# Batch norm and GELU per output block beside the matmuls, and a first expert search with two score buffers and indices in two halves

## The chip, the cores and the metric

The kernel runs on one NeuronCore of a Trainium2 chip. The metric is the device time of one execution in microseconds (us). TensorE (PE) does matmuls and transposes, VectorE (DVE) element work, maxima and index searches, ScalarE (ACT) activations and copies out of PSUM, GpSimd (POOL) issues the row gathers, and SyncE (SP) the plain transfers.

## The reference, cut to what matters

A graph of 1250 nodes with 512 features goes through four steps, each added to its input. The first two are where the change lies:

```python
# x: (1250, 512)
# 1: graph convolution, batch norm over the nodes, exact GELU
h = segment_sum(norm * (layernorm(x) @ W.T)[row], col) + b
h = (h - mean(h, 0)) * rsqrt(var(h, 0) + eps) * gamma + beta
x = x + gelu(h) + layernorm(x)
# 2: product-key experts, 8 heads, 256 + 256 keys, top 8
q1, q2 = halves of (layernorm(x) @ Wq + bq) per head
s1t, i1 = top_k(q1 @ keys1.T, 8);  s2t, i2 = top_k(q2 @ keys2.T, 8)
scores, best = top_k(all 64 sums of s1t and s2t, 8)
indices = i1 * 256 + i2 at best                 # 64 per node
vals = relu(x . w_down[indices]) * softmax(scores)
x = x + sum(vals * w_up[indices])
# 3: another graph convolution, 4: one of 8 matrices per node
```

## The kernel before, in words

The nodes are ten tiles of 128 rows (the last has 98). The engines run five hand-written programs, each in its own fixed order, which wait for each other through counting semaphores.

The graph convolution keeps its result transposed: `outT` has four blocks of 128 features (`o` = 0 to 3), each 1250 nodes wide. PE first makes four scaled sums `aggT` (four passes over the adjacency counts `AT`, L1312), then multiplies them by the weights, block by block, into one of two accumulators `acc` (L1357). ACT moves a whole block from PSUM to `outT` and adds the bias (L631); DVE takes the batch statistics (L931, L933). When all four blocks have them, the scale and the bias of the batch norm are worked out for the four at once (L934 to L944).

Between the sums and the blocks there is side work: DVE takes the self loops out of the ten tiles of `AT` (L925), ACT turns them into 16-bit copies `few` (L625, L627). On ACT this stands ahead of the first block's L631.

GELU runs by node tile: ACT computes four 128x128 pieces (L642) into `gt` or `diag`, PE flips them into a bank `TK` (L1367), DVE adds the bank to `x` (L950). Tile 0 goes first. Then comes the first search, with nothing between: the layer norm of tile 0 (`y`, L958 to L661), its flip, queries (`Q`, L1385), scores (`S`, L1396), copies of the scores to SBUF by ACT (L682), the eight largest and their places on DVE (L1003, L1008), and for all eight heads together the 64 sums, their best eight, and the 64 row numbers `idx` (L1017 to L1056), then the softmax. There is one score buffer `S` in PSUM for all heads, and two copies in SBUF (`sca`, `pick`). GELU of tiles 1 to 9 follows, after the search on all of ACT, PE and DVE.

The gathers are POOL's: for each tile 32 groups of two, each gather 128 rows of 4 KB out of `in_wdu` (L511). The ring has room for 11 groups; a slot is free again when PE has used it. POOL waits for the tile's `idx` before the first group. For each group DVE multiplies the rows with `y` (L1116), ACT makes a diagonal matrix of the result (L736), PE sums up (L1433). The search of tile 1 is laid over the groups of tile 0 by the table `FIRST`: its statistics, layer norm and queries begin after all ten tiles have their GELU, and its indices come in front of DVE's group 25. Those of the later tiles are laid over earlier groups of the tiles before, two ahead.

Of the kernel before, what the change touches and what calls it, by code (L numbers as in the profile page):

```python
# [111 lines left out]
def lay_out(nc, ctx, k):  # L112
    def sb(name, cols, dt=F32, rows=P):
        return ctx.enter_context(nc.sbuf_tensor(name, [rows, cols], dt))
# [155 lines left out]
    k.few0 = k.wide[:, 0:NPAD // 2].bitcast(I16)  # L270
    k.Y = [banks[2], banks[5]]
    k.O = [k.tr[0][:, :], k.tr[1][:, :]]

def program(nc, x_d, src_d, dst_d, w0t_d, par_d, wq_d, keys_d, wdu_d, w1_d, b1_d, we_d, out_d):
    k = Net()
    with ExitStack() as ctx:
# [3 lines left out]
        def sem(name):  # L283
            return ctx.enter_context(nc.semaphore(name))
# [185 lines left out]
def pool_program(pool, k):  # L470
# [90 lines left out]
def act_program(act, k):  # L561
# [72 lines left out]
    act.activation(k.bsd[:, :], k.bmv[:, FT:2 * FT], ACT.Sqrt, bias=k.eps[:, :]).then_inc(k.bnsd_ready, 1)  # L634
    act.wait_ge(k.bn_ready, 1)


    def gelu(i, par):
        if i > 1:
            act.wait_ge(k.tk_ready, i - 1)  # L640
        for o in range(FT):
            ins = act.activation(k.gtt[par][:, o * P:(o + 1) * P], k.outT[:, o * NPAD + i * P:o * NPAD + (i + 1) * P],  # L642
                                 ACT.Gelu, bias=k.bsc[:, FT + o:FT + o + 1], scale=k.bsc[:, o:o + 1])
        ins.then_inc(k.gelu_done, 1)

# [58 lines left out]
    def search_step(i, at, g):  # L704
        if g == at.y_root:
            y_root(i)
        if g == at.y_norm:
            y_norm(i)
        if g == at.y_copy:
            copy_yT(i)  # L710
        if g == at.y_keep:
            keep_y(i)
        if g in at.q_copy:
            copy_q(i, at.q_copy.index(g))
        if g in at.s_copy:
            copy_scores(i, at.s_copy.index(g))
        if g == at.exps:
            exps(i)
# [18 lines left out]
                                     scale=k.inner[:, j:j + 1])  # L737
            ins.then_inc(k.diag_ready, 1)

    gelu(0, 0)  # L740
    for g in range(FIRST.y_root, FIRST.exps + 1):
        search_step(0, FIRST, g)
    for i in range(1, NT):
        gelu(i, i % 2)
    for g in range(FIRST.y_root, 0):
        search_step(1, FIRST, g)
    for i in range(NT):
# [27 lines left out]
def dve_program(dve, k):  # L775
# [142 lines left out]
    for f in range(FT):  # L918
# [4 lines left out]
    for t in range(NT):  # L923
        loops = k.AT[:, t * NPAD + t * P:t * NPAD + (t + 1) * P]
        dve.tensor_tensor(loops, loops, k.ident[:, :], ALU.subtract).then_inc(k.unlooped, 1)  # L925
    dve.memset(k.outT[:, :].rearrange("p (o c) -> p o c", c=NPAD)[:, :, N:NPAD], 0.0)
    bmv = k.bmv[:, :].rearrange("p (c o) -> p o c", c=2)
    for o in range(FT):
        dve.wait_ge(k.outT_done, o + 1)
        for c, (c0, n) in enumerate(CHUNKS):  # L930
            dve.bn_stats(k.bst[:, (o * 3 + c) * 6:(o * 3 + c + 1) * 6], k.outT[:, o * NPAD + c0:o * NPAD + c0 + n])  # L931
        dve.drain()
        dve.bn_aggr(bmv[:, o, :], k.bst[:, o * 18:(o + 1) * 18])  # L933
    dve.drain().then_inc(k.bnvar_ready, 1)  # L934
    dve.wait_ge(k.bnsd_ready, 1)
    dve.reciprocal(k.bsd[:, :], k.bsd[:, :])
    dve.wait_ge(k.par_in, 16)
    dve.drain()
    dve.tensor_tensor(k.bsc[:, 0:FT], k.bsd[:, :], k.par[:, FT:2 * FT], ALU.mult)
    dve.drain()  # L940
    dve.tensor_tensor(k.bsc[:, FT:2 * FT], k.bsc[:, 0:FT], k.bmv[:, 0:FT], ALU.mult)
    dve.drain()
    dve.tensor_tensor(k.bsc[:, FT:2 * FT], k.par[:, 2 * FT:3 * FT], k.bsc[:, FT:2 * FT], ALU.subtract)
    dve.drain().then_inc(k.bn_ready, 1)  # L944


    def add_gelu(i, par):
        dve.wait_ge(k.tk_ready, i + 1)
        tile = k.x[:, i * D:(i + 1) * D]
        dve.tensor_tensor(tile, tile, k.TK[par], ALU.add).then_inc(k.x1_done, 1)  # L950

    add_gelu(0, 0)
    dve.memset(k.tmv[:, :], 1.0)
    dve.drain()

# [114 lines left out]
    def search_step(i, at, g):  # L1070
        if g == at.y_stats:
            y_stats(i)
        if g == at.y_inv:
            y_inv(i)
        if g in at.maxes:
            maxes(i, at.maxes.index(g))
        if g in at.finds:
            finds(i, at.finds.index(g))
        if g == at.sums:
            sums()  # L1080
        if g == at.best:
            best()
        if g == at.place:
            place()
        if g == at.codes:
            codes()
        if g == at.match:
            match()
        if g == at.rows:
            rows()  # L1090
        if g == at.index:
            index(i)
        if g == at.softmax:
            softmax(i)
# [24 lines left out]
                    accum_out=k.inner[:, j:j + 1])  # L1119
            ins.then_inc(k.inner_ready, 1)  # L1120

    for g in range(FIRST.y_stats, FIRST.softmax + 1):
        search_step(0, FIRST, g)
    for i in range(1, NT):
        add_gelu(i, i % 2)
# [125 lines left out]
def pe_program(pe, k):  # L1251
# [88 lines left out]
    for f in range(1, FT):  # L1340
        if f >= 2:
            pe.wait_ge(k.aggT_done, f - 1)
        for t in range(NT):
            for c0, n in CHUNKS:
                ins = piece(f, f % 2, t, c0, n)
        ins.then_inc(k.agg_ready, 1)

    pe.wait_ge(k.w_in, 16)
    for o in range(FT):
        pe.wait_ge(k.aggT_done, FT - 1 if o == 0 else FT)  # L1350
        if o >= 2:
            pe.wait_ge(k.outT_done, o - 1)
# [6 lines left out]
        ins.then_inc(k.out_ready, 1)  # L1359


    def flip_gelu(i, par):
        pe.wait_ge(k.gelu_done, i + 1)
        if i > 1:
            pe.wait_ge(k.x1_done, i - 1)
        for o in range(FT):
            ins = pe.transpose(k.TK[par][:, o * P:(o + 1) * P], k.gtt[par][:, o * P:(o + 1) * P], ident)  # L1367
        ins.then_inc(k.tk_ready, 1)

    flip_gelu(0, 0)  # L1370
# [69 lines left out]
    for g in range(FIRST.y_flip, FIRST.scores[-1] + 1):  # L1440
        search_step(0, FIRST, g)
    for i in range(1, NT):
        flip_gelu(i, i % 2)
# [93 lines left out]
```

## Time and profile before

| | |
|---|---|
| median of three runs | 1358.37 us (1356.52 to 1358.50) |
| the profiled execution | 1359.03 us, span 1357.2 us |
| PE busy | 1161.3 us, 86% of the span |
| DVE busy | 943.7 us, 70% |
| ACT busy | 520.7 us, 38% |
| POOL busy | 654.3 us, 48% |
| mean granted clock of PE | 0.966 of full |

A row of a timeline gives the start, the busy time, the engine, the line of the program, what is written and read, and in brackets the idle time ahead of it with what ended it. Matmuls in 32 bit show as two records each, and the busy time of a merged row reaches from its first start to its last end.

### The profile page before, as it was taken

How to read it: one execution, taken by the hardware profiler on the slowest of the kernel's cores; microseconds unless marked ns; L12 is line 12 of the kernel's file. 1: busy time of each engine (PE TensorE's matmuls, PEld its weight loads, DVE VectorE, ACT ScalarE, POOL GpSimd, SP SyncE). 2: the span in 40 equal slices, each digit the busy share in tenths (PEclk: the TensorE clock that was granted, in tenths of full speed). 3: DMA queues.
4: the chain of work that ended last, by engine and by line, in shares of the span. 5: the costliest groups of instructions: out<-in, count | busy, mean ns of one | idle time of the engine just before them, and what ended most of it. 6: DMA issues, size and time to landing. Idle time of an engine off the chain costs nothing.

```text
span 1357.2 us, 16428 instructions
## 1 busy us (share of the span) xinstructions
PE 1161.3 (86%) x3844; PEld 566.4 (42%) x3845; DVE 943.7 (70%) x2771; ACT 520.7 (38%) x1280; POOL 654.3 (48%) x706
## 2 busy tenths in 40 slices
PE   0788889996499999899898999989999799889098
PEld 0444445554254444444444444444444233334043
DVE  4777785022669997887978879788797866665211
ACT  1677730053644544344344444434443333320010
POOL 2000000000376677777777776777767777530212
PEclk9999999997599999999999999999999999999599
DMA  8400000000399999999999999999999999943443
GB/s 344 171 1 0 1 1 0 0 0 0 125 410 409 370 409 409 410 408 409 409 408 410 409 409 409 409 409 409 409 409 401 410 409 409 406 159 144 181 149 117
DMA packets 105765, 378.76 MB, mean 279 GB/s; under 512 B 11824, under 2 KB 11826, under 8 KB 104536
## 3 DMA queue, kind: packets, MB, share of 16 engines
q0 software_dynamic: 94720, 343.40, 63.7%
q1 hardware_dynamic: 10968, 34.48, 6.9%
q8 instruction: 30, 0.49, 0.1%
q14 instruction: 47, 0.39, 0.1%
HBM read 359.53 MB, written 19.41 MB: 279 GB/s over the span
## 4 chain that ended last, share of the span: by engine, by line
PE 44%; DVE 15%; DMA 13%; POOL 11%; issue 8%; ACT 5%; DVEq 4%; ACTq 0%; POOLq 0%; SPq 0%
PE tr L1433 17%; DMA AT<-in_wdu,idx 7%; POOL big L511 6%; PE acc L1312 6%; DMA big<-in_wdu,idx 4%; PE acc L1292 4%; POOL AT L511 4%; PE acc L1410 4%; PE acc L1385 3%; DVE big L1116 3%; PE tr L1484 3%; PE tr L1460 3%; DVE outT L846 2%; PE acc L1396 2%; DVE AT L1116 2%
## 5 line engine op out<-in xcount | busy, mean ns | idle before, releaser
L511 POOL DMA_INDIRECT big<-in_wdu,idx x466 | 439.8, 944 | 500.5 <-DVE idx L1056 348.8
L1433 PE MATMUL tr<-big,diag 128*128 128x512 f32 x932 | 434.1, 602 | 34.1 <-ACT diag L736 33.7
L736 ACT ACTIVATE diag<-ident,inner 128x128 f32<-128x128 f32 x640 | 221.6, 393 | 472.0 <-DVE inner L1116 470.6
L1116 DVE CUSTOM_DVE_ANT_0 big<-big,acc,prob 128x512 f32<-128x512 f32 x466 | 327.6, 742 | 79.7 <-DMA big<-in_wdu,idx 78.4
L1433 PEld LDWEIGHTS tr<-big,diag 128*128 128x128 f32 x932 | 168.5, 190 | 258.1 <-issue 166.9
L511 POOL DMA_INDIRECT AT<-in_wdu,idx x174 | 168.7, 970 | 61.6 <-issue 48.7
L1433 PE MATMUL tr<-AT,diag 128*128 128x512 f32 x348 | 163.3, 602 | 8.9 <-ACT diag L736 8.8
L1292 PE MATMUL acc<-outT,diag 128*128 x612 | 120.4, 347 | 40.3 <-DVE outT L846 18.7
L1116 DVE CUSTOM_DVE_ANT_0 AT<-AT,acc,prob 128x512 f32<-128x512 f32 x174 | 122.4, 742 | 33.5 <-DMA AT<-in_wdu,idx 33.1
L846 DVE TENSOR_SCALAR outT<-big 128x1280 f16 x204 | 98.0, 548 | 34.8 <-PE acc L1292 30.0
L1433 PEld LDWEIGHTS tr<-AT,diag 128*128 128x128 f32 x348 | 62.7, 190 | 90.5 <-issue 62.2
L1292 PEld LDWEIGHTS acc<-outT,diag 128*128 x612 | 59.2, 97 | 98.3 <-issue 74.0
L1385 PEld LDWEIGHTS acc<-yT,qk 128*128 128x128 f32 x640 | 81.6, 202 | 19.7 <-issue 17.5
L1385 PE MATMUL acc<-yT,qk 128*128 128x128 f32 x640 | 84.4, 288 | 2.4 <-ACT yT L657 1.4
L1312 PE MATMUL acc<-AT,big 128*128 128x512 f32 (+1 forms) x240 | 84.6, 513 | 0.0
L580 ACT ACTIVATE gt<-big 128x128 f16 x204 | 64.7, 387 | 19.4 <-PE acc L1292 13.6
L1410 PE MATMUL acc<-wide,h1bc 128*128 128x512 f32 (+1 forms) x144 | 61.3, 521 | 4.3 <-issue 4.2
L1396 PE MATMUL acc<-qk,qT 64*128 64x256 f32 x320 | 57.9, 439 | 4.5 <-ACT sca L682 2.3
L1312 PEld LDWEIGHTS acc<-AT,big 128*128 128x128 f32 x240 | 45.4, 190 | 37.9 <-issue 37.3
L1116 DVE DVE_READ_ACCUMULATOR2_ANT inner<- 128x1 f32 x640 | 52.7, 82 | 0.0
L1235 DVE TENSOR_SCALAR pick<-x 128x1 int32<-128x1 f32 x14 | 2.2, 154 | 72.7 <-PE tr L1484 72.7
L1410 PE MATMUL acc<-wide,gt 128*128 128x512 f32 (+1 forms) x96 | 43.2, 544 | 9.4 <-issue 4.9
(234 smaller groups left out, 1056.5 us busy)
## 6 DMA issues: line engine op xcount, KB each, us to landing
sorted_rows<-big SPq DMA_DIRECT2D x8, 1280.0 KB, 17.4
big<-in_we SPq DMA_DIRECT2D x8, 1024.0 KB, 15.1
big<-in_wdu,idx POOLq DMA_INDIRECT x466, 10.6
x<-sorted_rows SPq DMA_DIRECT2D x14, 512.5 KB, 3.4
AT<-in_wdu,idx POOLq DMA_INDIRECT x174, 10.8
x<-in_x SPq DMA_DIRECT2D x1, 2304.0 KB
qk<-in_wq SPq DMA_DIRECT2D x1, 2048.0 KB, 19.8
big<-in_w0t SPq DMA_DIRECT2D x1, 1024.0 KB, 27.5
```

The lines of the kernel that those rows point to most:

```text
L511: pool.indirect_dma_start(out=k.slot[r * GS + s], out_offset=None, in_=k.wdu_d, in_offset=bass.IndirectOffsetOnAxis(ap=k.idx[i % 2][:, j:j ...
L580: act.activation(k.far[:, bass.ds(half + b * P, P)], k.iota[:, NPAD + t * P:NPAD + (t + 1) * P], ACT.Abs, bias=k.neg[:, bass.ds(q * BPS + ...
L736: ins = act.activation(k.diag[:, c * P:(c + 1) * P], k.ident[:, :], ACT.Relu, scale=k.inner[:, j:j + 1])
L846: dve.tensor_scalar(k.ohs[:, bass.ds(half + c * NPAD, NPAD)], k.iota[:, t * P:t * P + NPAD], k.key[:, bass.ds(q * BPS + c, 1)], None, ALU. ...
L1116: ins = dve.tensor_tensor_reduce(out=row, in0=row, in1=k.Y[i % 2], scale=k.prob[:, (i % 2) * HK + j:(i % 2) * HK + j + 1], scalar=0.0, op0 ...
L1292: ins = pe.matmul(acc[:, c0:c0 + n], k.ohb[:, bass.ds(quarter + b * P, P)], k.ohs[:, bass.ds(half + b * NPAD + c0, n)], start=begin and b ...
L1312: return pe.matmul(k.acc[s][:, c0:c0 + n], k.h0[:, t * D + f * P:t * D + (f + 1) * P], k.AT[:, t * NPAD + c0:t * NPAD + c0 + n], start=(t ...
L1385: ins = pe.matmul(k.Q[:, (h % 4) * P:(h % 4 + 1) * P], k.wq[:, f * H * P + h * P:f * H * P + (h + 1) * P], k.yT[:, f * P:(f + 1) * P], sta ...
L1396: ins = pe.matmul(k.S[:, c, 0:NK], k.qT[half, (h % 4) * P:(h % 4 + 1) * P], k.keys[half, h * NK:(h + 1) * NK], start=True, stop=True)
L1410: ins = pe.matmul(k.G[n % 2 if n >= TWO_BANKS else 0][:, 0:cols], k.h1[j % 3][:, f * P:(f + 1) * P], k.wide[:, at:at + cols], start=(j == ...
L1433: ins = pe.matmul(k.O[i % 2], k.diag[:, c:c + P], row, start=(g == 0 and s == 0), stop=(g == NG - 1 and s == GS - 1))
L1460: ins = pe.matmul(k.tr[t % 2][:, :], k.agg1[:, f * NPAD + t * P:f * NPAD + (t + 1) * P], k.w1[f], start=(f == 0), stop=(f == FT - 1))
```

## The change

It does six things.

1. The self loops are taken out of tile t as soon as PE's last pass over `AT` is through with that tile (semaphore `at_free`), not after all passes.
2. ACT moves each block out of PSUM in three chunks (512, 512 and 226 nodes), each released by its own matmuls; DVE takes the statistics of each as it comes.
3. Scale and bias of the batch norm are worked out for each block by itself, and GELU is applied to the whole block in place, 1280 wide. For the last block, GELU is cut into tile 0, tiles 1 to 3 and tiles 4 to 9.
4. PE flips blocks 0 to 2 of tiles 0 to 3 into four banks (`early`) before the last block is finished, and the last block after it. Tiles 4 to 9 are flipped after the first search, with no GELU left to do there.
5. In the first search, even heads use `S` and the copy by ACT, odd heads the new `S1` (two other banks), which DVE reads from PSUM directly. Queries and scores alternate, two heads at a time.
6. The indices of the first search come in two halves (`first_half`): heads 0 to 3 before DVE begins with heads 4 to 7. POOL starts its first 16 groups on the first half. The softmax input moves behind the second half.

```diff
     for i in range(NT):
-        pool.wait_ge(k.idx_ready, i + 1)
         for g in range(NG):
+            if g == 0:
+                pool.wait_ge(k.idx_ready, i + 2 if i else 1)
+            if i == 0 and g == NG // 2:
+                pool.wait_ge(k.idx_ready, 2)
...
-    for o in range(FT):
-        act.wait_ge(k.out_ready, o + 1)
-        act.activation(k.outT[:, o * NPAD:o * NPAD + N], k.acc[o % 2][:, 0:N], ACT.Identity,
-                       bias=k.par[:, o:o + 1]).then_inc(k.outT_done, 1)
-    act.wait_ge(k.bnvar_ready, 1)
+    def out_row(o):
+        for c, (c0, n) in enumerate(CHUNKS):
+            act.wait_ge(k.out_ready, 3 * o + c + 1)
+            act.activation(k.outT[:, o * NPAD + c0:o * NPAD + c0 + n], k.acc[o % 2][:, c0:c0 + n], ACT.Identity,
+                           bias=k.par[:, o:o + 1]).then_inc(k.outT_done, 1)
+        act.wait_ge(k.bnvar_ready, o + 1)
+        act.activation(k.bsd[:, o:o + 1], k.bmv[:, FT + o:FT + o + 1], ACT.Sqrt,
+                       bias=k.eps[:, :]).then_inc(k.bnsd_ready, 1)
+        act.wait_ge(k.bn_ready, o + 1)
+
+    def gelu(o, i0, i1):
+        piece = k.outT[:, o * NPAD + i0 * P:o * NPAD + i1 * P]
+        act.activation(piece, piece, ACT.Gelu, bias=k.bsc[:, FT + o:FT + o + 1],
+                       scale=k.bsc[:, o:o + 1]).then_inc(k.gelu_done, 1)
+
+    for o in range(FT - 1):
+        out_row(o)
+        gelu(o, 0, NT)
+    out_row(FT - 1)
+    gelu(FT - 1, 0, 1)
+    gelu(FT - 1, 1, 4)
+    gelu(FT - 1, 4, NT)
...
+    def unloop(t):
+        if t < NT - 1:
+            dve.wait_ge(k.at_free, t + 1)
...
+    y_stats(0)
+    y_inv(0)
+    for i in range(1, 4):
+        add_gelu(i)
+    first_pair(0)
+    first_pair(2)
+    first_half(0)
+    first_pair(4)
+    first_pair(6)
+    first_half(1)
...
+    softmax(0)
+    for i in range(4, NT):
+        add_gelu(i)
...
+    def first_scores(h):
+        pe.wait_ge(k.qT_done, h + 1)
+        if h == 1:
+            pe.wait_ge(k.x1_done, 4)
+        elif h % 2:
+            pe.wait_ge(k.topk_done, h - 1)
+        elif h:
+            pe.wait_ge(k.sc_ready, h // 2)
...
+    for c in range(4):
+        queries(0, c)
+        first_scores(2 * c)
+        first_scores(2 * c + 1)
+    pe.wait_ge(k.gelu_done, FT + 2)
+    for i in range(4, NT):
+        pe.wait_ge(k.x1_done, max(i - 1, 4))
+        flip_gelu(i, k.TK[i % 2], range(FT)).then_inc(k.tk_ready, 1)
     pe.wait_ge(k.x1_done, NT)
```

ACT at the last block, before (L631 is the move out of PSUM, L634 the root, L642 GELU, L649 the root of tile 0's layer norm):

```order
L631 ACTIVATE outT<-acc,par 128x1250 x4
L634 ACTIVATE bsd<-bmv,eps 128x4
L642 ACT_TABLE_LOAD
L642 ACTIVATE gt<-outT,bsc 128x128 x4
L649 ACT_TABLE_LOAD
```

ACT at the same place of the changed program (L638, L641, L647 and L660 answer to them):

```order
L638 ACTIVATE outT<-acc,par 128x512 x2
L638 ACTIVATE outT<-acc,par 128x226
L641 ACT_TABLE_LOAD
L641 ACTIVATE bsd<-bmv,eps 128x1
L647 ACT_TABLE_LOAD
L647 ACTIVATE outT<-outT,bsc 128x128
L647 ACTIVATE outT<-outT,bsc 128x384
L647 ACTIVATE outT<-outT,bsc 128x768
L660 ACT_TABLE_LOAD
```

GELU and its table loads moved ahead into the blocks; the nine tiles' GELU that stood behind the first search is gone there. Both the root and GELU now need a table load in each of the last three blocks.

DVE in the first search, before: the tail of the last head (L1003, L1008), the index work for eight heads (L1017 to L1056), and the nine additions of GELU (L950).

```order
L1003 MAX top<-pick 128x8 x2
L1008 MAX_INDEX topi<-top,pick 128x8 x2
L1017 TENSOR_TENSOR pick<-top 128x512
L1018 CAST topf<-topi 128x128
L1023 MAX best<-pick 128x8 x8
L1028 MAX_INDEX pos<-best,pick 128x8 x8
```

DVE in the changed program at head 3 (`acc` is `S1` in PSUM) and the first half:

```order
L1168 MAX top<-acc 128x8 x2
L1171 MAX_INDEX topi<-top,acc 128x8 x2
L1185 TENSOR_TENSOR pick<-top 128x256
L1187 CAST topf<-topi 128x64
L1191 MAX best<-pick 128x8 x4
L1194 MAX_INDEX pos<-best,pick 128x8 x4
```

The same index work now stands twice, after head 3 and after head 7, with half the width or half the count each.

PE in the first search, before (L1385 queries, L1396 scores, L1367 flips of GELU):

```order
L1376 MATMUL acc<-ident,y 128x128 x4
L1385 MATMUL acc<-yT,qk 128x128 x16
L1396 MATMUL acc<-qk,qT 128x256 x4
L1385 MATMUL acc<-yT,qk 128x128 x8
L1396 MATMUL acc<-qk,qT 128x256 x2
```

PE there in the changed program (L1498 queries, L1563 scores):

```order
L1489 MATMUL acc<-ident,y 128x128 x4
L1498 MATMUL acc<-yT,qk 128x128 x8
L1563 MATMUL acc<-qk,qT 128x256 x4
L1498 MATMUL acc<-yT,qk 128x128 x8
L1563 MATMUL acc<-qk,qT 128x256 x4
```

The first scores now follow the first group of queries; before, the second group of queries stood between them.

## Rows read from the trace of the kernel before

**Rows 1.** The page, DMA queues: packets, MB, share of 16 engines

```profile
q0 software_dynamic: 94720, 343.40, 63.7%
```

**Rows 2.** Timeline of POOL: first gather, tile 1's first, the last

```profile
358.73 1.20 POOL L511 DMA_INDIRECT big<-in_wdu,idx  x1 [348.80 <-DVE idx L1056]
...
444.58 0.94 POOL L511 DMA_INDIRECT AT<-in_wdu,idx  x1 [6.13 <-DVE idx L1056]
...
1179.61 0.94 POOL L511 DMA_INDIRECT big<-in_wdu,idx  x1 [0.31 <-issue]
```

**Rows 3.** Windows: span, PE, PEld, DVE, ACT, POOL busy, clock, DMA, GB/s

```profile
380.00:438.00 58.00, 57.03 (x215) 28.75 (x214) 44.85 (x161) 24.60 (x68) 43.83 (x47) 1.00 1.03 409
438.00:458.00 20.00, 18.81 (x71) 9.39 (x69) 19.23 (x60) 10.52 (x25) 10.80 (x12) 1.00 0.92 342
458.00:1180.00 722.00, 672.56 (x2032) 311.93 (x2032) 595.90 (x1909) 294.05 (x772) 537.08 (x565) 1.00 1.03 409
```

**Rows 4.** Timeline of DVE from the last indices of search 0 on

```profile
359.21 0.69 DVE L950 TENSOR_TENSOR x<-x,tr 128x512 f32<-128x512 f32 x1
...
371.04 0.69 DVE L950 TENSOR_TENSOR x<-x,tr 128x512 f32<-128x512 f32 x1 [0.85 <-PE tr L1367]
...
373.52 0.75 DVE L1116 CUSTOM_DVE_ANT_0 big<-big,acc,prob 128x512 f32<-128x512 f32 x1
...
386.62 0.76 DVE L1003 MAX8 top<-sca 128x8 f32<-128x256 f32 x2 [7.67 <-ACT sca L682]
...
444.09 0.22 DVE L1056 SCALAR_TENSOR_TENSOR idx<-iab 128x64 int32<-128x64 f32 x1
```

**Rows 5.** Timeline of ACT, from the first block to tile 0's layer norm

```profile
292.18 2.48 ACT L631 ACTIVATE outT<-acc,par 128x1250 f32<-128x1250 f32 x2
...
310.67 1.30 ACT L631 ACTIVATE outT<-acc,par 128x1250 f32<-128x1250 f32 x1 [7.09 <-PE acc L1357]
313.96 0.30 ACT L634 ACTIVATE bsd<-bmv,eps 128x4 f32<-128x4 f32 x1 [1.99 <-DVEq L934]
314.27 1.28 ACT L642 ACT_TABLE_LOAD   x1
315.57 1.65 ACT L642 ACTIVATE gt<-outT,bsc 128x128 f32<-128x128 f32 x4
...
320.95 0.81 ACT L661 ACTIVATE y<-x,yco 128x512 f32<-128x512 f32 x1 [0.47 <-DVE yco L967]
```

**Rows 6.** Timeline of PE, blocks and first search

```profile
293.61 17.02 PE L1357 MATMUL acc<-big 128*128 128x512 f32 x48 [0.92 <-ACT outT L631]
317.27 1.11 PE L1367 MATMUL tr<-ident,gt 128*128 128x128 f32 x4 [6.64 <-ACT gt L642]
...
323.62 3.78 PE L1385 MATMUL acc<-yT,qk 128*128 128x128 f32 x16 [0.69 <-ACT yT L657]
328.21 3.75 PE L1385 MATMUL acc<-yT,qk 128*128 128x128 f32 x16 [0.81 <-ACT qT L675]
...
334.15 2.05 PE L1385 MATMUL acc<-yT,qk 128*128 128x128 f32 x16
...
346.52 1.23 PE L1396 MATMUL acc<-qk,qT 64*128 64x256 f32 x4 [0.78 <-ACT sca L682]
```

**Rows 7.** Windows around the granted clock (columns as in rows 3)

```profile
316.00:332.00 16.00, 9.80 (x42) 8.51 (x42) 1.90 (x6) 5.50 (x11) 0.00 (x0) 0.50 0.00 0
333.00:342.00 9.00, 6.67 (x48) 4.99 (x48) 5.86 (x22) 3.54 (x9) 0.00 (x0) 1.00 0.00 1
343.00:380.00 37.00, 18.01 (x69) 11.94 (x67) 27.12 (x89) 22.82 (x49) 16.25 (x17) 0.50 0.51 190
```

**Rows 8.** Timeline of DVE, two heads and the index work

```profile
333.41 0.75 DVE L1003 MAX8 top<-sca 128x8 f32<-128x256 f32 x2 [12.49 <-ACT sca L682]
...
335.05 0.74 DVE L1003 MAX8 top<-pick 128x8 f32<-128x256 f32 x2
...
350.22 0.69 DVE L1017 TENSOR_TENSOR pick<-top 128x512 f32<-128x512 f32 x1
...
358.20 0.23 DVE L1056 SCALAR_TENSOR_TENSOR idx<-iab 128x64 int32<-128x64 f32 x1
```

More of the change, by code:

```diff
@@ L200, in lay_out @@
     k.bsc = sb("bsc", 2 * FT)
+    k.bnm = sb("bnm", FT)
     k.tst = sb("tst", 12)
@@ L666, in keep_y @@
             act.wait_ge(k.inner_ready, (i - 1) * NG)
+        elif i:
+            act.wait_ge(k.topk_done, H)
+        else:
+            act.wait_ge(k.x1_done, 4)
         act.activation(k.Y[i % 2], k.x[:, i * D:(i + 1) * D], ACT.Identity, bias=k.yco[:, i % 2 * 2 + 1:i % 2 * 2 + 2],
@@ L738, in tile @@
             ins.then_inc(k.diag_ready, 1)
[L740 to L744, printed above, removed]
+    def first_scores(h):
+        act.wait_ge(k.s_ready, h + 1)
+        if h >= 4:
+            act.wait_ge(k.topk_done, h - 3)
+        act.activation(k.sc[h // 2 % 2].rearrange("p (c n) -> p c n", c=2), k.S[:, :, 0:NK], copy).then_inc(k.sc_ready, 1)
+    y_root(0)
+    y_norm(0)
+    copy_yT(0)
+    for c in range(4):
+        copy_q(0, c)
+        first_scores(2 * c)
+    keep_y(0)
+    exps(0)
     for g in range(FIRST.y_root, 0):
@@ L917, in dve_program, with scaled_sums @@
     dve.wait_ge(k.dinvB_ready, 2)
-    for f in range(FT):
+    def scaled_sums(f):
         dve.wait_ge(k.agg_ready, f + 1)
@@ L935, in dve_program @@
[L935 to L947, printed above, removed]
+        dve.bn_aggr(bmv[:, o, :], k.bst[:, o * 18:(o + 1) * 18]).then_inc(k.bnvar_ready, 1)
@@ L948, in add_gelu @@
+        dve.drain().then_inc(k.bn_ready, 1)
+    def add_gelu(i):
         dve.wait_ge(k.tk_ready, i + 1)
         tile = k.x[:, i * D:(i + 1) * D]
-        dve.tensor_tensor(tile, tile, k.TK[par], ALU.add).then_inc(k.x1_done, 1)
-    add_gelu(0, 0)
+        dve.tensor_tensor(tile, tile, k.early[i] if i < 4 else k.TK[i % 2], ALU.add).then_inc(k.x1_done, 1)
+    add_gelu(0)
     dve.memset(k.tmv[:, :], 1.0)
@@ L1120, in tile, with first_pair @@
             ins.then_inc(k.inner_ready, 1)
[L1122 to L1125, printed above, removed]
+    def first_pair(h):
+        dve.wait_ge(k.sc_ready, h // 2 + 1)
+        both = k.sc[h // 2 % 2]
+        for c in range(2):
+            dve.max(k.top[:, c * HK + h * 8:c * HK + h * 8 + 8], both[:, c * NK:(c + 1) * NK])
+        dve.drain()
+        for c in range(2):
+            ins = dve.max_index(k.topi[:, c * HK + h * 8:c * HK + h * 8 + 8],
+                                k.top[:, c * HK + h * 8:c * HK + h * 8 + 8], both[:, c * NK:(c + 1) * NK])
+        ins.then_inc(k.topk_done, 1)
+        h = h + 1
+        dve.wait_ge(k.s_ready, h + 1)
+        for c in range(2):
+            dve.max(k.top[:, c * HK + h * 8:c * HK + h * 8 + 8], k.S1[c])
+        dve.drain()
+        for c in range(2):
+            ins = dve.max_index(k.topi[:, c * HK + h * 8:c * HK + h * 8 + 8],
+                                k.top[:, c * HK + h * 8:c * HK + h * 8 + 8], k.S1[c])
+        ins.then_inc(k.topk_done, 1)
@@ L1345, in pe_program @@
                 ins = piece(f, f % 2, t, c0, n)
-        ins.then_inc(k.agg_ready, 1)
+            if f == FT - 1 and t < NT - 1:
+                ins.then_inc(k.at_free, 1)
+        if f < FT - 1:
+            ins.then_inc(k.agg_ready, 1)
+    ins.then_inc(k.agg_ready, 1)
     pe.wait_ge(k.w_in, 16)
@@ L1358, in pe_program, with flip_gelu @@
                                 k.aggT[:, f * NPAD + c0:f * NPAD + c0 + n], start=(f == 0), stop=(f == FT - 1))
[L1359 to L1370, printed above, removed]
+                if f == FT - 1:
+                    ins.then_inc(k.out_ready, 1)
+    def flip_gelu(i, bank, rows):
+        for o in rows:
+            ins = pe.transpose(bank[:, o * P:(o + 1) * P], k.outT[:, o * NPAD + i * P:o * NPAD + (i + 1) * P], ident)
+        return ins
+    pe.wait_ge(k.gelu_done, FT - 1)
+    for i in range(4):
+        flip_gelu(i, k.early[i], range(FT - 1))
+    for i in range(4):
+        pe.wait_ge(k.gelu_done, FT + 1 if i else FT)
+        flip_gelu(i, k.early[i], range(FT - 1, FT)).then_inc(k.tk_ready, 1)
     def flip_y(i):
@@ L1439, in pe_program, with first_scores @@
     pe.sem_inc(k.grp_done, RING)
[L1440 to L1443, printed above, removed]
+    def first_scores(h):
+        pe.wait_ge(k.qT_done, h + 1)
[5 more added lines that the diff above has]
+            pe.wait_ge(k.sc_ready, h // 2)
+        for c in range(2):
+            half = slice(64 * c, 64 * c + 64)
+            ins = pe.matmul(k.S1[c] if h % 2 else k.S[:, c, 0:NK], k.qT[half, (h % 4) * P:(h % 4 + 1) * P],
+                            k.keys[half, h * NK:(h + 1) * NK], start=True, stop=True)
+        ins.then_inc(k.s_ready, 1)
+    flip_y(0)
+    for c in range(4):
+        queries(0, c)
+        first_scores(2 * c)
+        first_scores(2 * c + 1)
[3 more added lines that the diff above has]
+        flip_gelu(i, k.TK[i % 2], range(FT)).then_inc(k.tk_ready, 1)
     pe.wait_ge(k.x1_done, NT)
```

79 lines of the change are left out of this document (64 added, 15 removed).

## The prediction, as it was made

> **What bounds the kernel now.** I read the page's queues first. Gathers move 343.4 MB [rows 1], so I asked when they start, when they stop and whether they pause. POOL's timeline says: first gather at 358.73, tile 1's first at 444.58 after a wait of 6.13 for its indices, the last at 1179.61 [rows 2]. From 444.58 on that is 575 steps in 735.0 us, 1.278 each. The windows show the DMA share at 1.03 and 409 GB/s from 458 to 1180 [rows 3]: that stage is bound by the gathers. Nothing this change touches lies after it, so the end moves with the moment at which tile 1's gathers begin. The reader is to see the hole before it: at 438 to 458 the rate is only 342, because tile 0's gathers had run out and tile 1's indices were not there.
>
> Next, what sets that moment. Tile 1's indices end on DVE at 444.31. Tile 0's first group starts on DVE at 373.52 [rows 4]. Between them lie 70.8 us in which DVE never waited for a gather: it waited for scores of search 1, 7.67 the longest. This stretch is unchanged code. So **the end follows T1, the start of DVE's first group, and not T0, the start of the gathers**. T0 gets earlier too, and that is worth nothing beyond T1's gain as long as tile 1's indices are what POOL waits for.
>
> So the sum is the shift of T1 = 373.52. Its chain is: blocks on PE, last batch norm and GELU, layer norm of tile 0, search, softmax, GELU of nine tiles, statistics of tile 1.
>
> **The blocks: -0.92.** PE stalled 0.92 before block 2, since ACT moved block 0 out only at 292.18, after the self-loop work [rows 5, 6]. In the new order that work runs under PE's last pass. What hides the new per-block work on ACT is PE, with 8.4 us per block (two in 17.02 with their tail [rows 6]); ACT needs after a block's last chunk 0.35 for the chunk, 1.28 load, 0.3 root, 1.28 load and GELU of 1280. The trace has no GELU that wide. Of 128 columns take 1.65 [rows 5], hence 0.39 each, so ten such pieces are 3.9, the upper bound; with 512 columns in 0.81 [rows 5], the slope is 0.87 ns per column, hence 1.5. I take 1.5: ACT is done 5 us after the block, the next block's first chunk comes 7.1 after it (8.4 less the last two chunks, 1.3). Slack 2; with 3.9 the overrun of 0.4 is caught up before the last chunk. PE ends at 310.63 - 0.92 = 309.71.
>
> **Last block to tile 0's layer norm: -2.9.** Before, PE's end to the root's start was 3.33 (310.63 to 313.96 [rows 5]). Now the last chunk is out at +0.5 and its statistics at about +1.6, but the table load for the root, which can only start at +0.5, ends at +1.8: I take 1.8, saving 1.5. Root to GELU stays 1.6. Before, GELU's start to `y` was 5.38 (315.57 to 320.95). Now GELU of tile 0 is 0.39 instead of 1.65, but two wider pieces stand behind it on ACT, 0.61 and 1.03 by the slope above, then the load 1.28, and root to `y` 0.76: 4.04, saving 1.34. `y` starts at 317.15 instead of 320.95, 3.8 earlier in all.
>
> In the trace a table load takes 1.28 and GELU starts 0.02 after it ends (314.27 and 315.57 [rows 5]), so I charge 1.28 for each. The Trainium skill (ScalarE: Activation LUTs, "What ACT_TABLE_LOAD costs") gives 2.66 us for each switch, a drain of 1.38 in it, and its section on table sets says to do all of one set before switching; that speaks against this change, which makes ten loads of five before T1. By that figure, an estimate, the two loads of the last block would cost 2.8 more and the sum would be 1347.3. The trace does not agree: between 314.27 and 315.57 there is no room for a drain.
>
> **The search: -4.1.** Before, `y` to the indices was 37.5 (320.95 to 358.43 [rows 5, 8]). Now, with the clock low at first, as before: `y` to first queries 2.67 as before, queries 3.78, copy of one head 0.44, scores 1.20, copy and handover 0.69: DVE's first head at +8.8 (325.93). A head takes 1.64 on DVE (333.41 to 335.05 [rows 8]). Heads 2 and 3 wait for PE: scores 1, then queries, in which I let the clock rise midway, 2.6, copy, scores, copy: 330.83. Two heads (3.35) and half 0 follow. The half is not in the trace: the full work took 8.21 (350.22 to 358.43); lower bound half of it, 4.1, upper bound all of it, 8.2. The fixed part of an instruction is about 0.16 (512 columns 0.69, 64 columns 0.23 [rows 8]), with drains that gives 4.9, nearest the lower. Half 0 ends at 339.1, gathers start at 339.4. Heads 4 to 7 then run without waiting, 6.6, since PE is two pairs ahead, and half 1 ends at 350.55. Odd heads are read from PSUM, which no row shows for this operation: the addition L950 from PSUM takes 0.69 [rows 4], the one from SBUF 0.69 [rows 8], so I take nothing, with a bound of 2.4 (four copies of 0.6). In sum 33.4 instead of 37.5.
>
> On the clock: it was 0.50 (1.2 GHz) from 316 to 332, 1.00 (2.4 GHz) from 333 to 342, and 0.50 again to 380 [rows 7]. Queries take 3.78 at the lower level and 2.05 at the higher, four score records 1.23 at the lower [rows 6]. It fell after PE had stopped at 310.63, and rose in the second group of queries, not in the first, which a gap of 0.81 followed. PE is again nearly idle after its flips, so I start low, and let it rise in the second group.
>
> **Indices to T1: -6.0.** Before: softmax 0.78, then nine additions paced by ACT's GELU, 359.21 to 371.73, then 1.79 to the first group [rows 4]: 15.1. Now: softmax input and exponent are no longer hidden, 0.6 more; tiles 1 to 3 were added long before, under PE's first queries; six additions, two at once, then four paced by flips of 1.11 (low clock [rows 6]): 5.9; then 1.79. Together 9.05, T1 = 359.6.
>
> **Sum:** 0.92 + 2.88 + 4.1 + 6.0 = 13.9. The profiled execution took 1359.03, so 1345.1; the median is 0.66 below that execution: **1344.5**. Ring: 22 gathers fit before the first group is consumed, 27 us of work from 339.4, while PE frees slots from T1 + 8 = 368 on; POOL stands for a microsecond or two, and after that is paced by tile 0's groups, each landed long before DVE's turn. Tile 1's gathers begin at 444.58 - 13.9 = 430.7. The two other queues are not involved; SP's transfers here are done.
>
> **The rivals.**
> (a) *The clock is high through the first search* (0.12). For: PE's pause before it is shorter and broken by flips. Against: the single flip groups at 358 to 371 left it at 0.50 [rows 7]. Queries lose 1.8, the second group 0.6, scores and flips 1.8, final flips 1.3: gain 19.4, 1339.0.
> (b) *The clock stays low through it* (0.13), since two gaps per pair remain. Each pair then costs PE 6.7 against DVE's 3.3; head 2 comes 1.5 and head 6 another 1.5 later: gain 10.9, 1347.5.
> (c) *A switch holds ACT for longer than the load that shows* (0.04). Now every block ends in two switches, and the two of the last block lie on the path; at twice 1.28 each they cost 2.6 more: gain 11.3, 1347.1. Against: the 0.02 behind the load of before [rows 5]. This is the skill's rule (section "Table sets: the hidden batching unit") as a mechanism of this kernel.
> (d) *The unseen operations cost their upper bounds* (0.05): PSUM reads 2.4, half 0 3.3 more (half 1 too, 6.6): with both for the most part, gain about 8, 1350.4.
> (e) *The gathers' start decides* (0.03): T0 19.3 earlier, and the 3.3 us hole of 438 to 458 (20 us at 342 of 409) closed too: 1335.8. Against: tile 1's indices already come 6.13 late, with a shorter lead.
> (f) *Slower* (0.04): in tile 0's groups PE is busy 57.03 of 58 us at full clock [rows 3]. If after T1 the clock does not rise, as it did at 380, each low microsecond costs half of one; from 28 low microseconds on the 13.9 are gone, and 60 of them give 1361. Against: the queries of tile 1 stand in front in both.
> (g) *Nothing* (0.03): the freed time turns up as a longer wait at tile 1's search; 1358.
>
> **How the numbers follow.** My case has 0.56, with 1342 to 1347 as its own spread. The range 1338.5 to 1350.5 takes in mine and (a) to (d), and leaves out (e) to (g), 1 in 10, with some 1 in 10 for what I mis-timed. A measurement of this kernel can tell 0.2%, 2.7 us: faster 0.93, same 0.03, slower 0.04.
>
> **What would show it.** PE's blocks end near 309.7 with no gap; `y` at 317; first gather at 339 to 340; tile 0's first group on DVE at 360; in front of tile 1's first gather a wait of about 10 us, longer than the 6.13 of before, at 430.7; then 735 us to the last gather. I am wrong if DVE waits for gathers in tile 0, if the 70.8 us from T1 to tile 1's indices stretch, or if a GELU in the blocks holds PE up.

## The result and the profile after

The changed kernel took 1344.2 us (median of 4 runs, 1342.44 to 1346.07) beside 1357.89 for the kernel before (4 runs, 1356.52 to 1358.5): ratio 0.9901 [0.9884, 0.9918], 13.7 us faster. The forecast was 1344.5. The profiled execution took 1342.44, and its span is 1340.5.

**POOL's timeline after**, as in [rows 2] (first gather, tile 1's first, the last):

```profile
336.79 1.20 POOL L517 DMA_INDIRECT big<-in_wdu,idx  x1 [326.88 <-DVE idx L1213]
...
427.64 0.94 POOL L517 DMA_INDIRECT AT<-in_wdu,idx  x1 [6.13 <-DVE idx L1089]
...
1161.82 0.94 POOL L517 DMA_INDIRECT big<-in_wdu,idx  x1 [0.30 <-issue]
```

The first gather is 21.9 us earlier, tile 1's first 16.9, the last 17.8. From tile 1's first to the last are 734.2 us, 735.0 before.

**Windows after**, columns as in [rows 3], with the same stages shifted:

```profile
363.00:421.00 58.00, 57.07 (x216) 28.86 (x215) 44.74 (x161) 24.59 (x68) 40.60 (x43) 1.00 1.01 392
424.00:444.00 20.00, 18.81 (x61) 8.39 (x60) 19.24 (x62) 11.21 (x29) 12.39 (x14) 1.00 0.79 285
444.00:1163.00 719.00, 670.57 (x2025) 310.49 (x2024) 593.33 (x1899) 292.65 (x769) 532.99 (x563) 1.00 1.03 409
```

The hole in front of tile 1's gathers has grown: 285 GB/s over 20 us, which is 6.1 us of transfer at 409, against 3.3 us at 342 before. A second, smaller hole lies earlier, behind the full slots of tile 0: from 380 to 400 the rate is 361, 2.3 us of transfer. The stage behind both is as it was.

**DVE's timeline after**, as in [rows 4, 8]: first head, half 0 of the index work (first and last row), half 1's last row, the additions, the first group, tile 1's indices:

```profile
324.41 0.76 DVE L1159 MAX8 top<-sca 128x8 f32<-128x256 f32 x2 [6.17 <-ACT sca L759]
...
326.04 0.74 DVE L1168 MAX8 top<-acc 128x8 f32<-128x256 f32 x2
...
331.43 0.42 DVE L1185 TENSOR_TENSOR pick<-top 128x256 f32<-128x256 f32 x1
...
336.29 0.19 DVE L1213 SCALAR_TENSOR_TENSOR idx<-iab 128x32 int32<-128x32 f32 x1
...
348.05 0.19 DVE L1213 SCALAR_TENSOR_TENSOR idx<-iab 128x32 int32<-128x32 f32 x1
...
349.57 1.29 DVE L983 TENSOR_TENSOR x<-x,tr 128x512 f32<-128x512 f32 x2
...
354.21 0.69 DVE L983 TENSOR_TENSOR x<-x,tr 128x512 f32<-128x512 f32 x1 [0.17 <-PE tr L1476]
...
356.70 0.75 DVE L1149 CUSTOM_DVE_ANT_0 big<-big,acc,prob 128x512 f32<-128x512 f32 x1
...
427.14 0.23 DVE L1089 SCALAR_TENSOR_TENSOR idx<-iab 128x64 int32<-128x64 f32 x1
```

**ACT's timeline after**, the last block to `y` (as [rows 5]):

```profile
308.44 1.03 ACT L638 ACTIVATE outT<-acc,par 128x512 f32<-128x512 f32 x2 [0.17 <-PE acc L1468]
309.48 1.28 ACT L641 ACT_TABLE_LOAD   x1
310.78 0.29 ACT L641 ACTIVATE bsd<-bmv,eps 128x1 f32<-128x1 f32 x1
311.09 1.28 ACT L647 ACT_TABLE_LOAD   x1
312.39 2.01 ACT L647 ACTIVATE outT<-outT,bsc 128x128 f32<-128x128 f32 x3
314.42 1.28 ACT L660 ACT_TABLE_LOAD   x1
315.71 0.29 ACT L660 ACTIVATE tsd<-tmv,eps 128x1 f32<-128x1 f32 x1
316.48 0.81 ACT L672 ACTIVATE y<-x,yco 128x512 f32<-128x512 f32 x1 [0.47 <-DVE yco L1000]
```

**PE's timeline after** (as [rows 6]): all four blocks, then the first queries.

```profile
275.05 33.74 PE L1468 MATMUL acc<-big 128*128 128x512 f32 x96
...
319.15 3.42 PE L1498 MATMUL acc<-yT,qk 128*128 128x128 f32 x16 [0.69 <-ACT yT L668]
...
324.09 2.05 PE L1498 MATMUL acc<-yT,qk 128*128 128x128 f32 x16
```

The four blocks are one row without a gap.

### The profile page after: what moved, and what is told of

It reads as the page before. It is cut to its first block, busy times and chain, and to the rows that moved or that the text cites. A ratio compares the mean times of both kernels' runs of the same rounds, so it can differ in the third digit from the quotient of the medians.

```text
span 1340.5 us, 16439 instructions
## 1 busy us (share of the span) xinstructions
PE 1154.5 (86%) x3844; PEld 563.0 (42%) x3845; DVE 947.6 (71%) x2792; ACT 518.2 (39%) x1258; POOL 652.3 (49%) x706
## 4 chain that ended last, share of the span: by engine, by line
PE 45%; DMA 15%; DVE 15%; POOL 11%; issue 8%; DVEq 3%; ACT 2%; ACTq 0%; POOLq 0%; SPq 0%
PE tr L1546 16%; POOL big L517 7%; DMA big<-in_wdu,idx 7%; PE acc L1419 6%; DMA AT<-in_wdu,idx 6%; PE acc L1399 5%; PE acc L1523 4%; DVE big L1149 3%; POOL AT L517 3%; PE acc L1498 3%; PE tr L1616 3%; PE tr L1592 3%; PE acc L1468 2%; DVE outT L870 2%; DVE AT L1149 2%
## 5 line engine op out<-in xcount | busy, mean ns | idle before, releaser
L1498 PEld LDWEIGHTS acc<-yT,qk 128*128 128x128 f32 x640 | 79.7, 198 | 18.7 <-issue 16.6
L1498 PE MATMUL acc<-yT,qk 128*128 128x128 f32 x640 | 82.3, 284 | 1.4 <-ACT yT L668 1.4
L1509 PE MATMUL acc<-qk,qT 64*128 64x256 f32 x288 | 50.6, 428 | 0.0
```

Source lines behind the costliest of these rows:

```text
L1498: ins = pe.matmul(k.Q[:, (h % 4) * P:(h % 4 + 1) * P], k.wq[:, f * H * P + h * P:f * H * P + (h + 1) * P], k.yT[:, f * P:(f + 1) * P], sta ...
L1509: ins = pe.matmul(k.S[:, c, 0:NK], k.qT[half, (h % 4) * P:(h % 4 + 1) * P], k.keys[half, h * NK:(h + 1) * NK], start=True, stop=True)
```

## The experiments

**The theories.** Theory A is that of the prediction: the end moves with T1, DVE's first group of tile 0, by way of tile 1's indices; an earlier first gather (T0) is worth nothing by itself. Theory B is rival (e): T0 decides, microsecond for microsecond. Theory D was formed after the second set and stands in the expectations from the third set on: two moments compete, called the two clocks below (they have nothing to do with PE's clock). The last gather is issued at the later of (first gather + 819) and (tile 1's first gather + 735).

These runs were made on three chips, and two of them are of another kind than the one above (1357.89): the kernel before took 1474.84 (18 runs) and 1475.15 us (17 runs) there, 1358.87 (9 runs) on the third. The kernel before has no trace on the slower kind. Ratios are with the kernel before on the same chip; differences between experiments are taken within one set.

### First set, on a chip with 1474.84 us for the kernel before

**The changed kernel again**, no edit.

> The changed kernel once more, as the measure for the runs beside it. Both theories: 0.990 of the kernel before, span 1340 to 1345. If the first rise of PE's clock in the first search (322 in the first trace) is what differs from run to run, this trace shows it at another place, and DVE's first group (356.7 there) moves by up to 3 us with it.

1456.08 us, ratio 0.9892 [0.986, 0.9923]. The ratio is that of the other chip, but the profile is not: its span is 1452.7, far outside the 1340 to 1345 expected. POOL's timeline:

```profile
375.31 0.94 POOL L517 DMA_INDIRECT big<-in_wdu,idx  x1 [11.01 <-PE tr L1546]
...
442.06 0.94 POOL L517 DMA_INDIRECT AT<-in_wdu,idx  x1 [3.35 <-DVE idx L1089]
```

The first gather is at 336.90, as above, but in DVE's additions stands a wait that no instruction of the kernel explains:

```profile
363.86 0.69 DVE L983 TENSOR_TENSOR x<-x,tr 128x512 f32<-128x512 f32 x1 [7.80 <-remote]
```

Such a wait is called a pause below. T1 comes at 366.34 instead of 356.70, POOL stands 11.01 before the 23rd gather since no slot is free, and from 470 to 1100 the rate is 360 GB/s.

**Gathers late.** POOL waits for both halves before tile 0's first gather. The search is unchanged, so T0 alone moves.

```diff
-                pool.wait_ge(k.idx_ready, i + 2 if i else 1)
+                pool.wait_ge(k.idx_ready, i + 2)
```

> The changed kernel, but POOL waits for both halves of the first indices before its first gather; nothing else moves. Theory A (the end follows DVE's first group and tile 1's indices, 70.7 us later): the first gather moves from 336.8 to 348.6, its 64 gathers are issued by 428.2, 0.8 after tile 1's indices, and the end moves by +0.5 to +1.5 us against the changed kernel. Rival B (the end follows the start of the gathers): +11.7 us.

1465.4, 0.9938 [0.9915, 0.9962]: 9.3 slower than the changed kernel, where A had 0.5 to 1.5. The first gather is 11.9 later (348.83). T1 at 356.97 is free of the pause, but a wait of 13.36 (remote) follows on ACT at 360.95, and tile 1's gathers begin at 452.39.

**Index work in one piece** behind head 7, with POOL waiting for it (its part of the edit is left out here).

```diff
     first_pair(2)
-    first_half(0)
     first_pair(4)
     first_pair(6)
-    first_half(1)
+    sums()
+    best()
...
+    index(0)
```

> The changed kernel with the first indices in one piece after head 7 (the functions of the search for the other tiles), the exponent hidden again. DVE does 8.2 us of index work instead of 10.2 and 0.5 less waiting, so its first group comes 2.4 earlier; the first gather comes 9.8 later. Theory A: -1.0 to -2.4 us against the changed kernel (-1.2 if POOL's 79.6 us of issuing for tile 0 then end last). Rival B: +9.8 us.

1465.09, 0.9927 [0.9904, 0.9949]: 9.0 slower, where A had a gain of 1.0 to 2.4. The first gather is at 348.44, T1 at 356.05. Two kernels with T0 late and T1 early both lose 9, against what A expected. But in both the pause had also moved, behind T1, so this chip could not separate T0 from the pause. The traces say where the time went: tile 1's first gather came at 452.39 and 450.31 instead of 442.06, and from there to the last gather are 837.0 and 836.8 us, 836.2 in the changed kernel. A's step from T1 to tile 1's indices is what did not hold here, 95.2 us with late gathers instead of 75.5.

**Index work of tile 1's search in one place of the schedule.** Six of its parts move into the place of the first, `sums`, ahead of group 19; the exponent moves to the next.

```diff
+FIRST.best = FIRST.place = FIRST.codes = FIRST.match = FIRST.rows = FIRST.index = FIRST.sums
+FIRST.exps = FIRST.sums + 1
```

> The changed kernel, but tile 1's index work stands in one piece ahead of group 19 of tile 0 instead of being spread over groups 19 to 25; same work. Its indices come six groups, some 8 us, earlier, before tile 0's gathers are all issued (421.5), and the wait of 6.13 in front of tile 1's first gather goes. Theory A: -5 to -6 us against the changed kernel. Rival C (DVE, 92% busy in this stretch, is the bound and not the gathers): 0 to -1 us. Rival B: 0.

1460.81, 0.9914 [0.9883, 0.9944]. Tile 1's indices are written at 434.18 and POOL waits for them no more, but for a free slot: 6.13 before 440.23. The 5 to 6 that A expected did not come. The median is 4.7 above the changed kernel's, but the intervals overlap, so no loss is shown either. Tile 1's first gather, at 445.20, is not earlier than the 442.06 of the changed kernel.

### Second set, on a chip with 1358.87 us

**The changed kernel, a third time.**

> The changed kernel a third time, as the measure for the runs beside it, since the second time came from a chip on which gathers, and engines in places, ran slower (409 GB/s and no unexplained pause before, some 358 there). If this chip is like the first: 1342 to 1346. Where the last call's pauses (idle time that the trace puts down to nothing it shows) come back, the time is over 1400.

1343.75, 0.9889 [0.9874, 0.9904], with the same steps as in the profile above: first gather 337.59, T1 357.49, tile 1's first 428.71 after 6.12, the last 1163.58; 280 GB/s from 424 to 444 and 363 from 380 to 400:

```profile
380.00:400.00 20.00, 20.00 (x75) 9.61 (x73) 16.07 (x57) 9.91 (x26) 13.50 (x15) 1.00 0.98 363
424.00:444.00 20.00, 18.82 (x69) 9.04 (x68) 19.25 (x61) 11.66 (x30) 11.62 (x13) 1.00 0.79 280
```

**Gathers late, here**: the edit of the first set.

> Again POOL waits for both halves before its first gather. Last time it cost +9.3 us of the 11.7 by which the gathers started later, on a chip whose gathers ran below 409 GB/s: there rival B held. Theory A, for a chip at 409 GB/s: +0.5 to +1.5 us against the changed kernel of this call. Rival B: +9 to +12.

1349.59, 0.9934 [0.992, 0.9947]: **5.8 slower**, neither A's 0.5 to 1.5 nor B's 9 to 12. T1 is 358.37 and tile 1's indices are written at 429.60, each some 1 us later than in the third run of the changed kernel. POOL's timeline and the window around tile 1's start:

```profile
350.21 1.20 POOL L517 DMA_INDIRECT big<-in_wdu,idx  x1 [340.30 <-DVE idx L1213]
...
1168.99 0.94 POOL L517 DMA_INDIRECT big<-in_wdu,idx  x1 [0.31 <-issue]
```

```profile
424.00:444.00 20.00, 18.81 (x74) 9.49 (x72) 19.24 (x61) 10.52 (x25) 15.16 (x16) 1.00 1.03 409
```

No hole is left: from the first gather to the last are 818.8 us for 639 steps, 1.281 each. POOL could issue one every 1.24, the DMA takes one every 1.28. So T0, 12.6 us apart in the two kernels, was worth less than 12.6: the early start had left the hole of 6.3 (20 us at 280 of 409), and lost another 2.3 behind full slots (20 us at 363 from 380 on). That leaves 4.0; the last gather moved by 5.4 and the time by 5.8, so 1.4 is not accounted for by these windows.

**The search of before in the changed kernel**: the blocks' part of the change alone. The first search runs from its old schedule (`search_step(0, FIRST, g)`, all heads copied by ACT, indices in one piece).

> The changed kernel with its first search as before (one score buffer in PSUM, all heads copied by ACT, indices in one piece, exponent hidden); batch norm and GELU by block stay. This is the first half of the change alone. From the layer norm of tile 0 to DVE's first group it should take 37.5 + 8.0 us where the changed kernel took 31.8 + 8.5: theory A: +5.2 us against the changed kernel, so some 8.5 of 13.7 us of the gain are the blocks' and 5.2 the search's. Rival B: gathers start at 354 instead of 336.8, +17, and nearly nothing of the gain is left.

1353.91, 0.9961 [0.9948, 0.9975]: 10.2 slower than the changed kernel, where A had 5.2 and B 17, and 5.0 faster than before. POOL:

```profile
354.90 1.20 POOL L515 DMA_INDIRECT big<-in_wdu,idx  x1 [344.98 <-DVE idx L1081]
...
1173.44 0.94 POOL L515 DMA_INDIRECT big<-in_wdu,idx  x1 [0.30 <-issue]
```

T1 is at 362.86, 10.7 earlier than in the trace of before, and by A the kernel should have won that. It won 5.0, with T0 only 3.8 earlier. Neither theory fits. From the first to the last gather are 818.5 again, as with late gathers.

**PE kept busy** in its idle time around the search by 14 matmuls of 512 columns whose results nothing reads.

```diff
+    def warm(n, bank):
+        for _ in range(n):
+            pe.matmul(bank, ident, k.keys[:, 0:512], start=True, stop=True)
...
```

> The changed kernel with 14 matmuls of 512 columns whose results nobody reads, in PE's idle time: 3 before and 3 after the last flips ahead of tile 0's layer norm, 5 behind the flip of tile 5, 3 behind that of tile 9. The granted clock should be 1.00 where it was 0.50 (315 to 322, and 339 to 363). Theory A with the clock as a cost on its path: first queries 2.05 instead of 3.42, flips 0.6 instead of 1.1, tile 1's first queries 2.05 instead of 3.73: -3 to -4.5 us against the changed kernel. If the clock there is not on the path: 0; if the added matmuls hold PE up: +1 to +3.

1341.75, 0.9876 [0.9861, 0.9891], the lowest median of all. It is 2.0 less than the changed kernel's, where 3 to 4.5 was expected; the two intervals overlap, though the slowest of the 4 runs (1342.16) lies below the fastest of the changed kernel (1342.38). Window of this kernel, columns as in [rows 3]:

```profile
340.00:360.00 20.00, 17.39 (x63) 10.05 (x62) 17.35 (x57) 5.49 (x12) 15.12 (x17) 0.81 1.01 387
```

The granted clock there is 0.81 instead of 0.59 in the changed kernel of this set. T1 is 2.9 earlier (354.58), tile 1's first gather 5.3 (423.43), the last 5.6 (1157.95). The profiled span is 4.0 shorter, the median of all runs 2.0 lower.

### Third set, on a chip with 1475.15 us

**Tile 1's index work in one place, again.** 

> Tile 1's index work in one piece ahead of group 19 again, if possible on a chip at 409 GB/s. After the last call I hold theory D: the last gather is issued at the later of two times, first gather + 819 us (640 gathers at 1.28) and tile 1's first gather + 734.5. In the changed kernel the second decides (336.8 + 819 = 1155.8 against 1161.8). Here tile 1's indices come some 8 us earlier, so the first decides: last gather near 1156, -6 us against the changed kernel (1344), 1338. Rival C (DVE is the bound): 0 to -1 us. On a chip with gathers below 409 GB/s: no gain, as in the first try.

1460.44, 0.9894 [0.9873, 0.9915]. Tile 1's indices are written at 437.89. The ratio is that of the changed kernel in the first set (0.9892): again no gain.

**The same with the 14 matmuls.** 

> The two edits together, the 14 unread matmuls and the compact index work. Theory D: the first gather at 335.4 as with the matmuls alone, last gather at 335.4 + 819 = 1154.4, some 1336.5, -7.4 us against the changed kernel. If the two only add up as single gains, -8. If the ring decides (22 gathers last 28 us, DVE's first group comes 19 after the first gather and frees a slot 8 later): -6.

1463.66, 0.9912 [0.9886, 0.9938], T1 at 369.56: no gain over the run before, where D had some 1.5 for a chip at 409 GB/s. Neither of these two forecasts of D could be tested, since this chip is of the slower kind.

**The self-loop work behind the last pass** instead of between the blocks' sums.

```diff
-    for f in range(FT - 1):
+    for f in range(FT):
         scaled_sums(f)
-    for t in range(NT - 1):
+    for t in range(NT):
         unloop(t)
-    scaled_sums(FT - 1)
-    unloop(NT - 1)
```

> The changed kernel with the self loops taken out after PE's last pass, as before; nothing else. ACT then moves block 0 out only at some 292, PE stands about 0.9 us before block 2, and every later step comes that much later: +0.9 to +1.5 us against the changed kernel. If ACT, now with GELU in each block, falls behind by more than its slack of 2 us: up to +4.

1463.03, 0.9895 [0.9867, 0.9922]: inconclusive in time. PE's timeline has the stall again that [rows 6] had with 0.92, and `y` starts at 318.38 instead of 316.3 to 317.4 in all other kernels with the new blocks:

```profile
293.66 17.03 PE L1464 MATMUL acc<-big 128*128 128x512 f32 x48 [1.22 <-ACT outT L638]
```

**The new first search in the kernel before**: the search's part alone.

> The kernel before with the new first search alone (two score buffers, indices in halves); batch norm for all blocks at once and GELU by tile, nine tiles of it behind the search on ACT, as before. First gather near 341 instead of 358.7, DVE's first group near 372 instead of 373.5, tile 1's first gather near 443. Theory D: last gather at 443.2 + 734.5 = 1177.7, -2 us against the kernel before. Rival B (the end follows the first gather): -17 us. If the halves of the change simply add: -10 (15.1 less the 5.0 of the blocks alone).

1474.49, 0.9991 [0.9975, 1.0007]: **no difference that can be told from nothing**. B's 17 and the 10 of halves that add up are outside the interval; D's 2 is inside it. POOL:

```profile
341.91 1.20 POOL L515 DMA_INDIRECT big<-in_wdu,idx  x1 [332.00 <-DVE idx L1198]
...
391.32 0.94 POOL L515 DMA_INDIRECT big<-in_wdu,idx  x1 [22.00 <-PE tr L1523]
```

And ACT:

```profile
353.45 0.26 ACT L708 ACTIVATE sm<-sm 128x64 f32<-128x64 f32 x1 [10.07 <-issue]
353.72 1.28 ACT L646 ACT_TABLE_LOAD   x1
355.02 1.65 ACT L646 ACTIVATE diag<-outT,bsc 128x128 f32<-128x128 f32 x4
```

Its gathers start 16.8 before those of [rows 2], which are from the faster kind of chip. But the old order of ACT puts the exponent ahead of nine tiles of GELU, and the exponent now needs both halves: the GELU chain starts at 355.02, 0.84 before the 355.86 in the trace of the kernel before. T1 stays late (381.87, with a pause of 8.44 in it), the 22 slots are full at 369, and the DMA stands still from 375 to 390 (1 GB/s from 380 to 390). An earlier T0 without an earlier T1 only filled the slots here. The pause is on this kind of chip alone, so the size is not to be carried over.

## Why the prediction was right, and where its reason was not

**The total was right, partly by luck**: 13.9 forecast, 13.7 measured between medians, 15.1 in the second set. The sum was meant as the shift of T1, and T1 moved 16.8 between the two traces: 1.8 up to PE's end of the blocks (0.9 forecast), 2.6 from there to `y` (2.9), 5.7 in the search (4.1), 6.6 from the indices to T1 (6.0). So the sum was 2.9 too small, and the gain in time was about as much below the shift of T1. Between the two profiled executions the gain is 16.6; these lay 1.1 above and 1.8 below the medians of their kernels. No run shows why the medians are closer together.

**Blocks, 0.92.** The stall is gone, as forecast. PE ends at 308.79, another 0.92 earlier than the 309.71 forecast; 0.69 of this had come about before the blocks (they start at 275.05 instead of 275.74), which the sum did not have. The run with the late self-loop work shows the cause, a stall of 1.22. GELU of 1280 took 1.45 to 1.46 (1.5 taken).

**Last block to `y`.** 7.69 for 7.44 forecast, 10.32 before. Of the 0.25, 0.19 stands ahead of the root, which starts 1.99 behind PE's end instead of 1.8: ACT had the last chunk out 0.68 behind it (308.44 + 1.03), not 0.5.

**Rival (c)** is refuted: behind eight of the ten table loads before T1 the next ACTIVATE starts 0.01 to 0.02 later, as at 309.48, 311.09 and 314.42 above. The other two loads (336.66, 348.68) lie inside a wait of ACT and cost nothing. The Trainium skill (ScalarE: Activation LUTs, "What ACT_TABLE_LOAD costs") has a drain of 1.38 with each switch; the trace does not show one here, in front of a load or behind it (the chunk ends at 309.47, the load starts at 309.48).

**Search.** `y` to the indices 31.76 instead of 33.4 forecast. Half the index work took 5.05 and 5.15 (4.9 taken, 8.2 the whole). MAX8 from PSUM took 0.74 and FIND_INDEX8 0.42, as from SBUF: rival (d) falls. The gain over the forecast is PE's clock, less what the halves cost more: it rose at 322 to 323, at the end of the first queries (3.42 instead of 3.78), not midway in the second, and DVE's first head is at 324.41, 7.93 behind `y` instead of 8.8. The second queries took 2.05 instead of 2.6, and head 2 came 11.5 behind `y` instead of 13.7. Of these 2.2 the two halves took 0.4 back. The prediction had also read the trace of before wrongly: the second queries there took 3.75 (328.21 to 331.96, [rows 6]), all at the lower level, and the clock rose only behind them, with the scores. In the changed kernel it was up from 323 to 339 and fell while PE stood idle from 335.32 to 339.90, so rival (a), whose price had the final flips at the higher level too, is refuted, and so is (b).

**Indices to T1.** 8.46, forecast 9.05. In all T1 moved 16.8 in the profile, 2.9 more than forecast, and the time did not get all of it in the median.

**T1 to tile 1's indices**: 70.7 against 70.8. It did not stretch; (f) and (g) fall.

**A slip in rival (f)**: at half a microsecond each, 60 low microseconds cost 30, so the time would be some 1374, not 1361. The clock rose in time, and nothing hangs on it.

**What was wrong** is the step "T0 gets earlier too, and that is worth nothing beyond T1's gain as long as tile 1's indices are what POOL waits for". By D, in the trace of before the two clocks stood within 2 us: 358.73 + 819 = 1177.7 and 444.58 + 735 = 1179.6. POOL's wait of 6.13 cost the DMA only 3.3, since it still had gathers queued: POOL issues one in 1.24, the DMA finishes one in 1.28. In the changed kernel the same 6.13 cost 6.1: the DMA had already run short behind the full slots (361 GB/s from 380 to 400), so nearly nothing was queued when POOL stopped. By D, T1 alone could win about 2 before T0 took over; no run moved T1 without T0. It needed T0 as well, and the new T0 is so early that T1 decides again:

| | first gather + 819 | tile 1's first + 735 | last gather, measured |
|---|---|---|---|
| before | 1177.7 | 1179.6 | 1179.61 |
| changed | 1155.8 | 1162.6 | 1161.82 |
| changed, second set | 1156.6 | 1163.7 | 1163.58 |
| gathers late | 1169.2 | 1165.8 | 1168.99 |
| old search | 1173.9 | 1170.7 | 1173.44 |
| 14 matmuls | 1154.4 | 1158.4 | 1157.95 |

The 819 was taken from the run with late gathers and the 735 from the kernel before, so these two rows are no test. The run with the old search tests the 819, the two changed ones and the 14 matmuls test the 735; they come out within 0.8. So with T0 21.9 and T1 16.8 earlier the later clock had 17 to give, and A's sum held because T0 had moved further than T1. The parts do not add. On the faster kind the blocks alone gave 5.0 (0.4%) and both together 13.7 to 15.1 (1.0 to 1.1%). On the slower kind the search alone gave nothing that can be told (0.1%), and both together 18.8 (1.1%).

The forecast of "about 10 us" for the wait ahead of tile 1's gathers failed at another term, the slots of the ring: the wait was 6.13. The prediction had POOL stand "for a microsecond or two"; it stood five times, 0.6 to 1.5 us each, at 365, 371, 382, 388 and 404, so that tile 0's 64 gathers took 84.7 us to issue instead of 79.7. That is the whole 5.0 by which T0 had gained on tile 1's first gather. And my expectation for the late gathers was too low because it priced POOL's wait and POOL's 1.24, not the hole in the DMA and its 1.28.

**Left open.** The compact schedule, which brings tile 1's indices earlier, was tried only on the chips with pauses. With it stands the question whether DVE, not the gathers, would then be the bound. On a chip like the first it could win at most the hole of 6.1; this was not tried. The 2.0 of the 14 matmuls is a third of the 5.6 that the last gather moved; the time behind the last gather varied from 177.6 to 182.2 in the six profiles of this kind of chip, and what sets it was not looked into.

## What to carry to other kernels

Where a queue of transfers bounds the kernel, price a wait of its issuer by the hole in the transfer rate, not by the wait: here 6.13 us of waiting cost 3.3 before and 6.1 after. Ask for each of the moments that can hold the queue up (its start, the next batch's indices, the first free slot) when the last transfer would end by it alone; only the latest counts, and two that lie within 2 us of each other must move together. Halves of a change tried alone then say little about the whole: 0.4% and 0.1% made 1.0 to 1.1%.

## What the runs showed of the hardware

Two kinds of chips: the kernel before took 1357.89 us in the first measurement and 1358.87 in the second set, and 1475 on the chips of the first and the third. On the latter two the gathers run at 360 GB/s from 470 to 1100 instead of 409, although in the first trace of them they reach 409 to 412 from 350 to 365 too. And engines stand still there with nothing in the kernel that they wait for: DVE from about 353 to 363.86, but for one addition (first gather at 336.90), DVE and ACT from about 363 to 371.55 (first gather at 341.91), ACT from 360.95 to 374.31 (first gather at 348.83). That is 12 to 21 us after the first gather. What it is was not settled. From tile 1's first gather to the last are 835.6 to 838.0 us in all eight profiles of this kind, so the second clock of D holds there with its own length. The ratio of the changed kernel was the same on both kinds, 0.9889 to 0.9901.

PE's clock rose at another place than in the kernel before. Here it was at 0.50 up to 322 and at 1.00 from 323, 3 us after the first queries had begun. In the kernel before it was at 0.50 up to 332 and at 1.00 from 333 [rows 7], behind the second queries and 9 us after the first had begun. In both, PE had done only flips, with gaps of up to 6.6 us (before) and 3.3 us (here), between the blocks and the first queries, so these two traces do not tell beforehand where the rise falls.
